# Building a 256 x 256 weight matrix from 50,000 edges: collect the edges that count first, then build in rounds

## What is computed

```python
W = zeros(256, 256).at[src, dst].set(edge_weight)      # an edge with src or dst over 255 falls outside and is dropped
x = layernorm(x + x @ W)
for l in range(4):                                     # relational graph layer
    h = einsum('ni,rio->rno', X, weights[l])           # 4 relations
    agg = segment_sum(h[etype, src] / degree, dst)     # over the 50,000 edges
    out = layernorm(agg + X @ roots[l] + biases[l]) * gamma + beta
    X = elu(out) + X
return layernorm(x + X)
```

## Time and profile before

| what | value |
|---|---|
| median of 3 runs | 2713.06 us (2712.81 to 2717.09) |
| the profiled execution's own time | 2710.93 us |
| its span | 2709.2 us |
| mean granted clock of PE | 0.825 |
| PE busy | 2199.1 us (81%) |
| VectorE busy | 1557.3 us (57%) |
| POOL busy | 1512.8 us (56%) |
| ACT busy | 371.0 us (14%) |

### The profile page before, as it was taken

One profiled execution on the slowest core, in us unless ns is written; L12 is line 12 of the kernel. 1 busy time (PEld: TensorE's weight loads), 2 busy tenths in 40 slices (PEclk: granted clock), 3 DMA queues, 4 the chain that ended last, 5 costly groups with the idle time before them and its releaser, 6 DMA issues.

```text
span 2709.2 us, 45161 instructions
## 1 busy us (share of the span) xinstructions
PE 2199.1 (81%) x7889; PEld 1327.8 (49%) x7890; DVE 1557.3 (57%) x5264; ACT 371.0 (14%) x765; POOL 1512.8 (56%) x1591
## 2 busy tenths in 40 slices
PE   4668966778788889888898898988889968777776
PEld 2435444666344555434455563344455534445554
DVE  7988079997344566434455663344556623446676
ACT  2553400331000111100011110000111100000000
POOL 1000051003777777377777764777777567777773
PEclk9878965999678999867789996578899966777788
DMA  5000340001344444333444442334444343334342
GB/s 160 0 0 8 148 141 16 0 0 41 105 120 129 136 151 144 96 105 113 121 129 144 144 146 84 105 113 128 129 144 152 119 146 105 104 105 119 105 120 63
DMA packets 103215, 280.43 MB, mean 104 GB/s; under 512 B 27676, under 2 KB 39050, under 8 KB 102798
## 3 DMA queue, kind: packets, MB, share of 16 engines
q0 software_dynamic: 75264, 205.62, 26.4%
q10 hardware_dynamic: 18224, 62.59, 6.2%
q1 hardware_dynamic: 9566, 10.42, 1.3%
HBM read 219.61 MB, written 58.91 MB: 103 GB/s over the span
## 4 chain that ended last, share of the span: by engine, by line
PE 48%; issue 13%; DVE 13%; POOL 11%; DMA 9%; DVEq 3%; ACT 1%; POOLq 1%; ACTq 0%; SPq 0%
PE acc L465 26%; POOL ring L275 11%; DMA ring<-h_rows,idx 9%; PE hp L372 7%; PE pw L372 7%; PE acc L454 3%; DVE S L883 3%; PE acc L457 2%; PE pw L348 1%; DVE hot_s L856 1%; DVE ring L753 1%; DVE hot_n L856 1%; POOLq L181 1%; ACT XT L501 1%; PE tr L361 1%
## 5 line engine op out<-in xcount | busy, mean ns | idle before, releaser
L275 POOL DMA_INDIRECT ring<-h_rows,idx x1568 | 1505.2, 960 | 1156.1 <-issue 880.9
L465 PE MATMUL acc<-ring,S 128*128 x3712 | 1227.0, 471 | 196.8 <-SPq L228 144.7
L906 DVE TENSOR_SCALAR S<-iota,ecol 128x128 f32<-128x128 f32 x1856 | 610.4, 366 | 860.2 <-PE acc L465 739.2
L465 PEld LDWEIGHTS acc<-ring,S 128*128 128x128 f32 x3712 | 749.4, 223 | 666.0 <-issue 590.6
L372 PE MATMUL hp<-wts,XT 128*128 (+1 forms) x416 | 212.3, 658 | 22.4 <-ACT XT L501 22.4
L372 PE MATMUL pw<-wts,XT 128*128 (+1 forms) x384 | 196.9, 661 | 20.3 <-ACT XT L501 20.3
L454 PE MATMUL acc<-wts,XT 128*128 (+1 forms) x400 | 124.7, 441 | 62.3 <-issue 62.3
L564 ACT ACTIVATE work<-work 128x256 f32<-128x256 f32 x100 | 41.7, 417 | 908.8 <-DVE work L935 899.9
L856 DVE TENSOR_TENSOR hot_s<-iota,place 128x400 bf16<-128x400 f32 x196 | 111.4, 569 | 89.2 <-PE acc L415 84.9
L372 PEld LDWEIGHTS hp<-wts,XT 128*128 128x128 f32 x416 | 83.6, 212 | 120.4 <-issue 120.4
L454 PEld LDWEIGHTS acc<-wts,XT 128*128 128x128 f32 x400 | 83.5, 217 | 119.7 <-issue 109.9
(11 more groups left out here) (206 smaller groups left out, 1365.5 us busy)
## 6 DMA issues: line engine op xcount, KB each, us to landing
h_rows<-hst ACTq DMA_DIRECT2D x100, 512.0 KB, 3.1
ring<-h_rows,idx POOLq DMA_INDIRECT x1568, 2.8
wts<-weights SPq DMA_DIRECT2D x32, 128.0 KB, 3.1
x_rows<-X ACTq DMA_DIRECT2D x1, 3200.0 KB, 10.2
wts<-x_rows ACTq DMA_DIRECT2D x1, 3200.0 KB, 12.4
X<-x SPq DMA_DIRECT2D x1, 3072.0 KB
out<-X ACTq DMA_DIRECT2D x2, 1024.0 KB
wts<-roots SPq DMA_DIRECT2D x8, 128.0 KB, 2.9
```

Of the source, the lines that this page charges most:

```text
L275: pool.indirect_dma_start(ring[:, k, :], None, h_gather, bass.IndirectOffsetOnAxis(ap=idx[:, g * J + j:g * J + j + 1], axis=0)).then_inc(l ...
L465: nc.tensor.matmul(accs[t % 2][:, 0:D], S[:, at * J + j, :], ring[:, bass.ds((c + j) % SLOTS, 1), :].rearrange("p a d -> p (a d)"), start= ...
L906: v.tensor_scalar(S[:, at * J + j, :], iota[:, t * P:(t + 1) * P], dst_c[:, bass.ds(c + j, 1)], inv_c[:, bass.ds(c + j, 1)], ALU.is_equal, ...
```

## The change

An edge inside W gets a rank, its number among the inside edges in file order. VectorE marks inside edges (`inside`). PE sums the marks over partitions, once up to each partition (with `later`) and once over all (with `ones`). VectorE sums along the 392 columns in nine doubling steps (L824) and has the rank. Its low 7 bits are a slot (a partition), the rest a block.

A loop over the groups with `dst` under 256 (29 groups) then moves the edges' values: VectorE writes where block and slot match (`in_blk`, `to_slot`), POOL multiplies the block marks by five values of each edge, `src`, `dst+1` and three parts of the weight (`placed`), and PE moves them to slot and block by four small matmuls a group (`few_ps`). A window holds 12 blocks, 1,536 edges; the number of windows is worked out at run time.

Out of a window, W is built in three rounds of 512 edges over all 256 columns at once. In PE's program the key row of a round stands now behind the matmuls of the round before. The turning of x stands ahead of all that, two tiles at a time through `pw`. The split of the weights into three bf16 parts is POOL's. The table's masks `T_LO` and `T_SB` are no longer read.

```diff
+WB, WG = 12, 3
+VALS = 5
+MAXWIN = -(-E // (WB * P))
+PAD = 256
...
-            pool.wait_ge(s["w_mm"], 2)
+            pool.wait_ge(s["col_out"], 6)
+            pool.wait_ge(s["tab_ready"], 1)
+            pool.sem_inc(s["passed"], 1)
+            src_c, dst_all, w_c = (ecol[:, a, 0:NG, :].rearrange("p g j -> p (g j)") for a in (1, 0, 2))
+            nc.gpsimd.tensor_copy(vals[:, :, 0], src_c).then_inc(s["w_vals"], 1)
+            nc.gpsimd.tensor_scalar(vals[:, :, 1], dst_all, 1.0, None, ALU.add).then_inc(s["w_vals"], 1)
+            nc.gpsimd.tensor_copy(vals[:, :, 2], w_c).then_inc(split, 1)
...
+            windows, hi = windows_of(pool)
+            with pool.Fori(0, windows) as win:
+                base = window_base(pool, win)
+                with pool.Fori(0, hi) as g:
+                    n = base + g
+                    pool.wait_ge(s["w_few_mm"], n + 1)
+                    pool.wait_ge(s["w_in_blk"], n + 1)
+                    pool.sem_inc(s["passed"], 1)
+                    nc.gpsimd.tensor_tensor(placed[:, bass.ds(n % 2, 1), :, :, :].rearrange("p b j w v -> p (b j) w v"),
+                                            in_blk[:, bass.ds(n % 2, 1), :, :].rearrange("p b j w -> p (b j) w").unsqueeze(3).to_broadcast([P, J, WB, VALS]),
+                                            vals[:, bass.ds(g * J, J), :].unsqueeze(2).to_broadcast([P, J, WB, VALS]),
+                                            ALU.mult).then_inc(s["w_placed"], 1)
...
+            pe.wait_ge(s["w_inside"], 2)
+            nc.tensor.matmul(hp[0][:, 0:NC], later[:, 0:P], inside, start=True, stop=True)
+            nc.tensor.matmul(hp[1][:, 0:NC], ones[:], inside, start=True, stop=True).then_inc(s["w_prefix"], 1)
...
-            def key_row_out(q):
-                pe.wait_ge(s["key_masked"], q + 1)
-                nc.tensor.matmul(rowb[:], ones[0:NG, :], key_row, start=True, stop=True).then_inc(s["key_row_ready"], 1)
-            for t in range(KH):
-                lo_t, end_t, sb_t = tile_bounds(pe, t)
-                key_row_out(sb_t + lo_t + t)
-                with pe.Fori(lo_t, end_t) as g:
-                    w = sb_t + g
-                    pe.wait_ge(s["w_dup"], w * J + J)
-                    key_row_out(w + (t + 1))
+            def turn_x(u):
+                if u > 1:
+                    pe.wait_ge(s["xT_ready"], u - 1)
+                for i, t in enumerate(range(2 * u, min(2 * u + 2, NT))):
+                    for k in range(KH):
+                        m = nc.tensor.transpose(pw[:, u % 2, (2 * k + i) * P:(2 * k + i + 1) * P], X[:, t, k * P:(k + 1) * P], ident[:])
+                m.then_inc(s["x_tr"], 1)
+            pe.wait_ge(s["ld_x"], 32)
+            for u in range(-(-NT // 2)):
+                turn_x(u)
+            windows, hi = windows_of(pe)
+            few_ps, row_ps = tr[:, 0:WB * VALS], hp[0][0:WB * VALS, 0:P]
+            with pe.Fori(0, windows) as win:
+                base = window_base(pe, win)
+                pe.wait_ge(s["w_few"], win + 1)
+                pe.sem_inc(s["passed"], 1)
+                nc.tensor.matmul(few_ps, zeros[:, 0:P], zeros[:, 0:WB * VALS], start=True, stop=True)
+                with pe.Fori(0, hi) as g:
+                    n = base + g
+                    pe.wait_ge(s["w_to_slot"], n + 1)
+                    pe.wait_ge(s["w_placed"], n + 1)
+                    for j in range(J):
+                        m = nc.tensor.matmul(few_ps, to_slot[:, bass.ds(n % 2, 1), j, :].rearrange("p b n -> p (b n)"),
+                                             placed[:, bass.ds(n % 2, 1), j, :, :].rearrange("p b w v -> p (b w v)"),
+                                             start=False, stop=True, skip_group_check=True)
+                    m.then_inc(s["w_few_mm"], 1)
+                pe.wait_ge(s["w_few"], win + 2)
+                pe.sem_inc(s["passed"], 1)
+                nc.tensor.transpose(row_ps, few, ident[:]).then_inc(s["w_few_tr"], 1)
+                pe.wait_ge(s["w_few_row"], win + 1)
+                for q in range(WG):
+                    w = win * WG + q
+                    if q > 0:
+                        pe.wait_ge(s["w_dup"], win * (WG * J) + q * J)
+                    for j in range(J):
+                        b = q * J + j
+                        m = nc.tensor.matmul(rowb[:, j * P:(j + 1) * P], pick[:, b:b + 1].to_broadcast([WB * VALS, P]), few_row, start=True, stop=True)
+                    m.then_inc(s["w_key_row"], 1)
                     pe.wait_ge(s["w_src_hot"], w * J + 2 * J)
-                    pe.wait_ge(s["w_upd"], w * 2 + 2)
+                    pe.wait_ge(s["w_upd"], w * 2 + 1)
                     for c in range(3):
...
-                                m = nc.tensor.matmul(pw[:, k, 0 if c == 0 else P:2 * P], OS[:, j, k * P:(k + 1) * P], rhs,
+                                m = nc.tensor.matmul(pw[:, k, 0 if c == 0 else D:2 * D], OS[:, j, k * P:(k + 1) * P], rhs,
...
-            def turn_x(t):
-                if t > 0:
-                    pe.wait_ge(s["xT_ready"], t)
-                for k in range(KH):
-                    m = nc.tensor.transpose(rowb[:, k * P:(k + 1) * P], X[:, t, k * P:(k + 1) * P], ident[:])
-                m.then_inc(s["x_tr"], 1)
             def first_product(t):
 
                 if t > 1:
                     pe.wait_ge(s["y_ready"], t - 1)
-                pe.wait_ge(s["xT_ready"], t + 1)
                 for k in range(KH):
                     m = nc.tensor.matmul(accs[t % 2][:, 0:D], XT[:, k, columns_of(t)], Wm[:, k, :], start=k == 0, stop=k == KH - 1)
                 m.then_inc(s["x_mm"], 1)
 
             pe.wait_ge(s["w_ready"], 1)
-            pe.wait_ge(s["ld_x"], 32)
-            turn_x(0)
+            pe.wait_ge(s["xT_ready"], -(-NT // 2))
...
+            for u in range(-(-NT // 2)):
+                x_transposed(u)
+            windows, _ = windows_of(act)
+            with act.Fori(0, windows) as win:
+                act.wait_ge(s["w_few_tr"], win + 1)
+                act.sem_inc(s["passed"], 1)
+                nc.scalar.activation(few_row, hp[0][0:WB * VALS, 0:P], ACT.Copy).then_inc(s["w_few_row"], 1)
+                for q in range(WG):
+                    w = win * WG + q
+                    if q == 0:
+                        act.wait_ge(s["w_few"], win + 2)
                     act.wait_ge(s["w_src_hot"], w * J + J)
                     act.sem_inc(s["passed"], 1)
                     for j in range(J):
                         nc.scalar.activation(src_dist[:, j, :], iota[:, 0:D], ACT.Abs, scale=-1.0,
-                                             bias=ecol[:, 1, bass.ds(g, 1), j:j + 1].rearrange("p a j -> p (a j)")).then_inc(s["w_src_dist"], 1)
+                                             bias=few_v[:, q * J + j, 0:1]).then_inc(s["w_src_dist"], 1)
...
+                    dve.wait_ge(s["col_out"], 2)
+                    v.tensor_scalar(slot_c, src_col, float(D), None, ALU.is_lt).then_inc(s["w_inside"], 1)
+                    dve.wait_ge(s["w_inside"], 1)
+                    v.scalar_tensor_tensor(out=inside, in0=dst_col, scalar=float(D), in1=slot_c, op0=ALU.is_lt, op1=ALU.mult).then_inc(s["w_inside"], 1)
...
-            w_all = ecol[:, 3, 0:NG, :]
...
+            dve.wait_ge(s["w_prefix"], 1)
+            v.tensor_scalar(sums[0][:, PAD:PAD + NC], hp[1][:, 0:NC], 0.0, None, ALU.add).then_inc(s["w_sums"], 1)
+            for i in range(9):
+                a, b = sums[i % 2], sums[1 - i % 2]
+                dve.wait_ge(s["w_sums"], i + 1)
+                v.tensor_tensor(b[:, PAD:PAD + NC], a[:, PAD:PAD + NC], a[:, PAD - 2 ** i:PAD - 2 ** i + NC], ALU.add).then_inc(s["w_sums"], 1)
+            upto, rank_f = sums[1][:, PAD:PAD + NC], sums[0][:, PAD:PAD + NC]
+            dve.wait_ge(s["w_sums"], 10)
+            v.tensor_tensor(rank_f, upto, hp[0][:, 0:NC], ALU.add).then_inc(s["w_rank"], 1)
...
+            v.tensor_tensor(rank_i, rank_f, hp[1][:, 0:NC], ALU.subtract).then_inc(s["w_rank"], 1)
...
+            v.scalar_tensor_tensor(out=blk_c, in0=inside, scalar=float(-KEY), in1=blk_i, op0=ALU.mult, op1=ALU.add).then_inc(s["w_blk"], 1)
...
+            windows, hi = windows_of(dve)
+            with dve.Fori(0, windows) as win:
+                base = window_base(dve, win)
+                with dve.Fori(0, hi) as g:
+                    n = base + g
+                    dve.wait_ge(s["w_few_mm"], n + 1)
+                    dve.sem_inc(s["passed"], 1)
+                    v.tensor_tensor(in_blk[:, bass.ds(n % 2, 1), :, :].rearrange("p b j w -> p (b j) w"),
+                                            iota_b[:].unsqueeze(1).to_broadcast([P, J, WB]),
+                                            blk_c[:, bass.ds(g * J, J)].unsqueeze(2).to_broadcast([P, J, WB]),
+                                            ALU.is_equal).then_inc(s["w_in_blk"], 1)
+                    v.tensor_tensor(to_slot[:, bass.ds(n % 2, 1), :, :].rearrange("p b j n -> p (b j) n"),
```

(54 more changed lines are left out.)

146 lines of the change are left out of this document (86 added, 60 removed).

## The result

The changed kernel takes 2627.56 us, median of four runs (2626.74 to 2628.71), beside 2713.42 for the kernel before: a ratio of 0.9681, interval [0.9664, 0.9698], 85.9 us less. Forecast were 2605, with 2587 to 2640 as the range. Its profiled execution took 2628.71 us, with a span of 2626.9.

The account below looks back on a forecast made before the run. VectorE was taken to bound the building of W. W ready 104.9 us earlier plus 2.4 from first products gave 107.3 off 2710.9, 2603.6; with the median 2.1 above that execution, 2605, range 2587 to 2640.

Parts of the forecast that it names:

- The rank: VectorE's chain of dependent operations after the table: 10.2 us, ending at 45.4 us.
- 4.3 us in all ... under VectorE's cover: POOL's seven operations beside the rank: 4.3 us in all, hidden behind VectorE's work.
- Turning x: PE's early turns of x before the moving loop: PE arrives last, at 50.5 us, 2.8 behind VectorE.
- The moving loop: 29 groups over VectorE, POOL and PE at 1.1 us each: 32 us, ending at 82.5 us.
- three hand-overs of 0.15: Moving loop: signalling between engines, 0.15 us each, within a group's half ring of 0.96 us.
- registers and the branch may not all hide: Moving loop: allowance for register and branch work, raising a group from 0.96 to 1.1 us.
- Three rounds: Building W from the window: VectorE's 24.7 us plus 9.6 of waits on PE, 34.3 us, between 30 and 43.
- if the clock rises in the course of these longer bursts: Three rounds: condition on PE's clock under which VectorE's waits for matmuls and key rows total 9.6 us.
- POOL sets the pace: Rival, moving loop: POOL's operation costs what an issue does, 1.7 us a group, 17 more, 2622; chance 17%.
- Slow PE throughout: Rival, PE's clock: rounds take 43 us (+9) and x is turned late (+5), 2619; chance 7%.
- all covers hold: Rival: group 0.8 to 0.9 us, PE at 2.4 GHz in rounds and sooner in the loop, 2590; chance 12%.
- rival B: Layers behind W: the change makes them 5 us longer, so the kernel before again shows 2449 to 2450 us.

Follow-up runs that it names:

- the unrolled loop: Changed kernel with the moving loop's body written twice, with fixed buffer halves and 30 groups: ratio 0.9648 [0.9633, 0.9663] to the kernel before.
- the experiment: Changed kernel with x turned late again, tile by tile between the first products: ratio 0.969 [0.9674, 0.9706] to the kernel before.
- the last run: The kernel before, unchanged, profiled once more for the scatter of single profiles: 2708.98 us.

## Why the prediction was right, and where it was off

The sign and the place held: the end moved by what W moved. The size came out at 85.9 us where some 108 were forecast. That this still lies in the range is in part luck: the range kept 17 us for a slow POOL in the loop and 9 for slow rounds, and the loop used up 12 of them by a mechanism that no rival names. The step from the sum of 107.3 us to the 87.5 by which the first turned x of the layers came earlier (259.82 to 172.29) is a miss of 19.8. It splits along the prediction's own steps.

- *The table:* 35.2 forecast, 34.85 measured. Right.
- *The rank, 10.2 us:* measured 13.6 (34.89 to 48.45). The failed step is "4.3 us in all ... under VectorE's cover". POOL's seven took 10.0 us, not 4.3, and this cover was not free: the nine doublings took 9.56 us for 5.37 without POOL, 4.2 more. The other rows were as taken or shorter. The table reads were 3.1 for 2.3.
- *Turning x:* PE was to be last at 50.5. Its turns ended at 44.7, its reads and what else stands there took 5.4 us more, and it was there at 50.06; VectorE was last, at 51.56. The start of the loop was off by 1.1 only, since two errors met.
- *The moving loop, 32 us:* measured 44.0, 12.0 of the miss. The operations were right (VectorE 0.21 and 0.69, POOL 0.70 for 0.6, PE 0.69 for 0.67). The failed terms are "three hand-overs of 0.15" and the 0.14 for "registers and the branch may not all hide". The measured ring, (0.21 + 0.70 + 0.69 + 3h)/2 = 1.47, gives h = 0.45. With constant addresses PE followed POOL by 0.15, as assumed, and the group fell to 1.12, about the forecast 1.1. What was missing is the address work out of registers: it lengthened the hand-overs and kept PE at 1.36 us a group. PE's 0.67 was right by luck. It was taken from the counting loop, whose matmuls have 128 columns and constant buffer halves, no register among them; 60 columns with constants take 0.36, and the registers made 0.69 of that. The estimate with the Trainium skill's "GPSIMD Engine Reference", section 3.1, held for POOL's two-input operation, an estimate of 0.53 and a fixed part, against 0.59 to 0.71 measured, and 0.80 in the unrolled loop.
- *Window to rounds, 3:* 3.5.
- *Three rounds, 34.3:* 40.1, 5.8 of the miss. VectorE's own part was 24.7, just as forecast (6.8, 8.25, 8.26, 1.4). The waits were 5.57, 5.49 and 4.35, 15.4 for 9.6: behind VectorE's products the matmuls cost some 4.3 us each time where 2.0 was taken, the key rows 1.3 where 1.8 was. The failed term is "if the clock rises in the course of these longer bursts". It did rise, but only at the end of each: the granted clock was 0.50 (1.2 GHz) up to 109 us and 1.00 from 110, so that the key row was fast and the matmuls, at 6.0 to 6.5 us, were near the slow 7.1 (the rows doubled give 3.9 and 7.2, where I wrote 3.6 and 7.1).
- *First products, 2.4:* 2.04, and 2.1 by the experiment.

The rival "POOL sets the pace" gave 2622 and is nearest to the result in time, but its mechanism is refuted: POOL was idle half of the loop, and with four buffers it ran two groups ahead of PE while the pace stayed at 1.36 us. "Slow PE throughout" was half right, in the rounds; "all covers hold" failed in its two large terms, the 0.8 to 0.9 us group and PE at 2.4 GHz in the rounds.

Open: of the 87.5 us at the first turned x, 82.3 reached the end in the two profiles and 85.9 in the medians. From that point to the end the changed kernel's profile has 2454.6 us and those of its variants 2450.9 to 2458.0, the two of the kernel before 2449.4 and 2449.0. All ten profiles with the change lie above both without it, so a few us of the gain, 2 to 9, seem to be given back behind W, as rival B of the last run has it. No run isolates where or why, and on one chip whole executions of the kernel before lie up to 9.3 us apart.

## What to carry to other kernels

When short instructions form a ring over several engines, count the address work out of registers with the operations: here they were 1.60 of the ring's 2.94 us and the hand-overs the rest. Unroll to constant buffer halves before adding buffers. When a price is read from another loop, look whether its addresses are constants and how many columns it moves. Cover beside POOL is not free for VectorE where its operations have two inputs in SBUF; count both engines' time. When a round is made larger to have fewer of them, put the next round's small inputs ahead of this round's long matmuls on the in-order queue.
